# A transformer layer on one core: a new order of steps in the tail of attention, and products of ones while TensorE waits

## The chip, the cores and the metric

The kernel runs on one core of one Trainium2 chip. The metric is the device time of one execution in microseconds (us), smaller being better. PE is TensorE, DVE is VectorE, ACT is ScalarE, POOL is GpSimd and SP is SyncE, which here only starts transfers. All times in this document come from the profile of the kernel, from an answer of its trace, or from the times of whole executions.

## The reference, cut to what matters

One adaptive layer-norm block: linear attention over 2 sequences of 2048 tokens (16 heads of 16), and behind it a mixture of 8 experts of which each token wants 2, where each expert takes at most 1280 tokens, those with the largest weights first.

```python
h = _layernorm(x) * (1 + ca) + sa
x = x + ga * attention(h)        # q_feat, k_feat = elu + 1; kv = sum over tokens of k_feat x v
                                 # out = q_feat @ kv / max(q_feat @ k_sum, 1e-6) @ W_out
h = _layernorm(x) * (1 + cb) + sb
logits = xf @ router_w.T; probs = softmax(logits); topw, topi = top_k(probs, 2)
# tokens sorted by expert and weight; the first `capacity` (1280) of an expert are kept
g = einsum('ecd,edf->ecf', disp, wg); u = einsum('ecd,edf->ecf', disp, wu)
eo = einsum('ecf,efd->ecd', silu(g) * u, wd)
x = x + gb * scatter_add(eo * weight)
```

## The kernel before, in words

Every engine runs its own instruction list, written out by hand, and the lists meet at semaphores. An engine takes its instructions strictly in the order written, so an instruction that waits holds up all that stands behind it on its engine. TensorE's list, VectorE's list and so on are all emitted by a function `step(s)` of that engine, once for each step from -3 to 54. In a step each stage works on another tile of 128 tokens; there are 32 tiles (`NT`), 16 for a sequence (`TB`). The front half (layer norm, the products with `wqkv`, rotation, features, the sum `kv_ps` over keys and values) works on tile *step* or near it. The back half (called "attention proper" below) works `LAG` = 18 steps later, since it needs the sum over a whole sequence: in step *s* it does

- on PE: the transposes of `att` for tile *s*-19 (L1466), the product of `q_in` with `kvb` for tile *s*-18 (L1480), the router's product for tile *s*-21 (L1406), the output product into `y_ps` for tile *s*-19 (L1494), and the transposes of `x2` for tile *s*-20 (L1504);
- on DVE: `den_m`, `logits`, `den_r`, the greatest logits, `att` (L989), their places (`MAX_INDEX`, L883), `x2` = `y_ps` + `x_re` (L1003), and its mean and variance (L1005, L841, L846, L847);
- on ACT: the copies `attT` (L663) and `x2T` (L669) out of PSUM and the normalised tile `xn` (L678), which needs `rs2` and `sh2` from POOL;
- on POOL: `rs2` (L524), `sh2` (L526), and `xm`, `h2`.

From step 32 on only the back half is left. The second sequence's state `kvb[1]` is formed on DVE from `kv_ps` (L1033, L1035) at the end of step 33 and is first wanted by PE in step 34. The function `alone(s)` says from which step the back half has PSUM to itself: from there PE does the product L1480 ahead of the router's, the router's product gets a bank of its own, the transposes of `att` go to another bank than `y_ps` and so no longer wait for `x2`, and ACT copies `x2T` ahead of `xn` rather than behind it.

In the same steps DVE also does the softmax of the two best logits (`choice(g, part)`, parts 0 to 8) for the first 16 tiles (g = 0) and for the next 8 (g = 1). Part 0 writes `over`; ACT then takes its exponential (`exp_logits`, L608), at the end of its step `EX_STEPS`.

Behind attention stands a search with little work for PE: `choice(2, ...)` for the last 8 tiles, two transposes of the weights (L1513), 15 rounds (`DIGITS`) in which ACT and DVE count how many weights lie above a candidate (L698, L1060) and PE adds the counts over the partitions (L1518, L1520, L1522), then masks (L1533, L1534), the looking up of the chosen tokens (`look`, L1544, `place`, L1551), the gather of their rows by POOL (L556), in five parts for three groups of tiles, and their transposes (`transpose_x`, L1563). The first gate product (L1587) begins the experts, where PE is the bound.

## Time and profile before

| | us |
|---|---|
| median of 3 executions | 634.47 |
| lowest and highest | 633.26, 636.43 |
| the profiled execution | 630.97 |
| its span | 629.1 |
| granted TensorE clock in it, mean | 0.948 |
| PE busy | 559.4 (89%) |
| DVE busy | 453.0 (72%) |
| ACT busy | 322.9 (51%) |
| POOL busy | 269.9 (43%) |

The trace is that of one execution, which took 630.97 us; 1.87 us of it lie outside the span. PE's time is nearly the span, but the clock that it is granted is not full everywhere: 1.00 is 2.4 GHz and 0.50 is 1.2 GHz. So the profile is read by stretches: the front and back halves together up to about 157 us, attention proper alone up to 213 us, the search up to 264 us, and the experts.

### The profile page before, as it was taken

What the parts mean: (1) busy time and instruction counts of PE and PEld (TensorE: products, weight loads), DVE (VectorE), ACT (ScalarE), POOL (GpSimd) and SP (SyncE); (2) the same over time, 40 slices, a digit from 0 to 9 for tenths busy, and PEclk for the clock granted to TensorE, in tenths of its full rate; (3) what the DMA queues carried; (4) which work ended last, traced back from release to release, by engine and by line L of the source; (5) the groups of instructions that cost most, each with busy time, mean ns of one, the idle gap of its engine ahead of it and who ended that gap; (6) DMA issues with size and microseconds to landing.
All of it is one profiled execution on the core that took longest, in us unless ns stands there. A gap on an engine that the chain in (4) does not pass through costs nothing.

```text
span 629.1 us, 12912 instructions
## 1 busy us (share of the span) xinstructions
PE 559.4 (89%) x3895; PEld 519.9 (83%) x3895; DVE 453.0 (72%) x1357; ACT 322.9 (51%) x718; POOL 269.9 (43%) x406
## 2 busy tenths in 40 slices
PE   5999999999888532499999999999999999999993
PEld 4587779988677311399899999999999999999993
DVE  4688799998678887787577577677676776666441
ACT  4688878886334434045445454445445444454331
POOL 5788857776667600403044062070170260431321
PEclk9999999999889855599999999999999999999997
DMA  6322458644546470333637347258066174360312
GB/s 169 106 67 85 123 176 241 220 137 141 168 143 202 158 215 0 86 101 101 185 84 145 102 97 170 64 110 209 21 124 188 52 138 140 89 139 6 37 19 25
DMA packets 92480, 75.28 MB, mean 120 GB/s; under 512 B 12156, under 2 KB 89094, under 8 KB 92424
## 3 DMA queue, kind: packets, MB, share of 16 engines
q1 hardware_dynamic: 82344, 57.39, 30.5%
q0 software_dynamic: 8992, 15.90, 13.6%
q10 hardware_dynamic: 1088, 1.31, 0.7%
q8 instruction: 27, 0.44, 0.3%
q14 instruction: 29, 0.24, 0.1%
HBM read 52.41 MB, written 22.16 MB: 119 GB/s over the span
## 4 chain that ended last, share of the span: by engine, by line
PE 65%; DVE 10%; issue 4%; ACT 3%; POOL 2%; DMA 2%; SPq 0%; POOLq 0%; DVEq 0%; ACTq 0%
PE bank L1587 29%; PE bank L1601 14%; PE bank L1622 4%; PE bank L1369 4%; PE bank L1494 3%; PE bank L1637 2%; PE bank L1480 1%; PE bank L1563 1%; ACT side L698 1%; PE bank L1406 1%; DMA w_raw<-wd 1%; DVE st L1005 1%; DVE x L1003 1%; PE bank L1449 1%; PE bank L1544 1%
## 5 line engine op out<-in xcount | busy, mean ns | idle before, releaser
L556 POOL DMA_INDIRECT xg<-h_rows,g_idx x40 | 44.1, 1103 | 236.5 <-DVE g_idx L1186 226.7
L1587 PE MATMUL bank<-xT_h,w_h 128*128 128x320 f32 x448 | 139.9, 312 | 1.5 <-DVE xT_l L1215 1.5
L1587 PE MATMUL bank<-xT_l,w_h 128*128 128x320 f32 x448 | 138.4, 309 | 0.0
L1587 PE MATMUL bank<-xT_h,w_l 128*128 128x320 f32 x448 | 138.2, 309 | 0.0
L733 ACT CAST hid_h<-hid 128x320 fp32r<-128x320 f32 x112 | 51.5, 460 | 86.6 <-DVE hid L1243 86.6
L566 POOL DMA_INDIRECT out<-yo,s_idx x40 | 67.1, 1676 | 59.8 <-DVE yo L1308 26.7
L1587 PEld LDWEIGHTS bank<-xT_h,w_h 128*128 128x128 f32 x448 | 84.6, 189 | 2.2 <-issue 1.4
L729 ACT ACTIVATE act_g<-bank 128x320 f32<-128x320 f32 x112 | 49.0, 437 | 70.0 <-PE bank L1587 69.1
L1587 PEld LDWEIGHTS bank<-xT_l,w_h 128*128 128x128 f32 x448 | 84.5, 189 | 0.0
L1587 PEld LDWEIGHTS bank<-xT_h,w_l 128*128 128x128 f32 x448 | 84.4, 188 | 0.0
L1248 DVE TENSOR_TENSOR hid_l<-hid,hid_h 128x320 fp32r<-128x320 f32 x112 | 54.9, 490 | 36.5 <-ACT hid_h L733 36.1
L1601 PE MATMUL bank<-w_h,hid_h 128*128 128x256 f32 x280 | 80.2, 286 | 0.0
L1243 DVE TENSOR_TENSOR hid<-act_g,bank 128x320 f32<-128x320 f32 x112 | 54.4, 486 | 34.7 <-ACT act_g L729 33.4
L1601 PE MATMUL bank<-w_h,hid_l 128*128 128x256 f32 x280 | 78.1, 279 | 0.0
L1601 PE MATMUL bank<-w_l,hid_h 128*128 128x256 f32 x280 | 78.0, 279 | 0.0
L1201 DVE TENSOR_TENSOR w_l<-w_raw,w_h 128x768 fp32r<-128x768 f32 x64 | 61.2, 962 | 11.0 <-ACT w_h L706 10.4
L706 ACT CAST w_h<-w_raw 128x768 fp32r<-128x768 f32 x64 | 52.8, 832 | 2.1 <-DMA w_raw<-wd 2.1
L1369 PE MATMUL bank<-wqkv_h,hT_h 128*128 128x256 f32 (+1 forms) x128 | 49.0, 383 | 5.0 <-DVE hT_l L960 3.3
L1601 PEld LDWEIGHTS bank<-w_l,hid_h 128*128 128x128 f32 x280 | 52.9, 189 | 0.0
L1601 PEld LDWEIGHTS bank<-w_h,hid_l 128*128 128x128 f32 x280 | 52.8, 189 | 0.0
L1601 PEld LDWEIGHTS bank<-w_h,hid_h 128*128 128x128 f32 x280 | 52.7, 188 | 0.0
L542 POOL TENSOR_TENSOR rot<-rot_a,rot_b 128x512 f32<-128x512 f32 x32 | 42.2, 1318 | 12.4 <-DVE rot_b L953 11.9
(223 smaller groups left out, 1299.6 us busy)
## 6 DMA issues: line engine op xcount, KB each, us to landing
w_raw<-wg SPq DMA_DIRECT2D x32, 256.0 KB, 3.7
w_raw<-wu SPq DMA_DIRECT2D x32, 256.0 KB, 4.9
w_raw<-wd SPq DMA_DIRECT2D x16, 512.0 KB, 6.0
x_in<-x SPq DMA_DIRECT2D x32, 128.0 KB, 2.1
q_store<-qT SPq DMA_DIRECT2D x32, 128.0 KB, 2.1
q_in<-q_store SPq DMA_DIRECT2D x32, 128.0 KB, 2.2
x_re<-x SPq DMA_DIRECT2D x32, 128.0 KB, 2.1
out<-x SPq DMA_DIRECT2D x32, 128.0 KB, 2.1
```

Of the source, the lines that this page charges most:

```text
L542: nc.gpsimd.tensor_tensor(rot[s.par(0)][:, :], rot_a[:, :], rot_b[:, :], ALU.add).then_inc(rope_d, 1)
L556: nc.gpsimd.indirect_dma_start(out=xg[par][:, a, :], out_offset=None, in_=h2_rows, in_offset=bass.IndirectOffsetOnAxis(ap=g_idx[par][:, a: ...
L566: nc.gpsimd.indirect_dma_start(out=out_rows, out_offset=bass.IndirectOffsetOnAxis(ap=s_idx[par][:, a:a + 1], axis=0), in_=yo[:, a, :], in_ ...
L706: nc.scalar.copy(w_h[:, f, :], w_raw[:, f, :]).then_inc(sp_h, 1)
L729: nc.scalar.activation(act_g[h][:, 0:HCAP], bank[2 * h][:, 0:HCAP], ACT.Silu).then_inc(silu_d, 1)
L733: nc.scalar.copy(hid_h[f % 2][:, h * HCAP:(h + 1) * HCAP], hid[h][:, 0:HCAP]).then_inc(hh_d, 1)
L1201: V.tensor_tensor(w_l[:, f, :], w_raw[:, f, :], w_h[:, f, :].bitcast(F32), ALU.subtract).then_inc(sp_l, 1)
L1243: V.tensor_tensor(hid[h][:, 0:HCAP], act_g[h][:, 0:HCAP], bank[2 * h + 1][:, 0:HCAP], ALU.mult)\
L1248: V.tensor_tensor(hid_l[f % 2][:, h * HCAP:(h + 1) * HCAP], hid[h][:, 0:HCAP], hid_h[f % 2][:, h * HCAP:(h + 1) * HCAP].bitcast(F32), ALU. ...
L1369: ins = MM(out, x[j][:, k, :], w[i][:, k, cols], start=n == 0, stop=n == 3 * KC - 1)
L1587: last = MM(bank[2 * h + m][:, 0:HCAP], W[i][:, f, at:at + P], XT[j][:, k, cols], start=n == 0, stop=n == 3 * KC - 1)
L1601: last = MM(bank[4 + a // 2][:, a % 2 * D:(a % 2 + 1) * D], (hid_h, hid_l)[j][f % 2][:, a * P:(a + 1) * P], (w_h, w_l)[i][:, f, 4 * P:], s ...
```

## The change

1. `alone(s)` holds from step 34 (`NT + 2`) instead of step 38 (`NT + 6`).
2. The state `kvb[1]` is formed in step 33 right behind `att` instead of at the end of the step.
3. In every step of the back half `MAX_INDEX` stands behind the statistics of `x2` (`BN_STATS`) instead of ahead of `x2`.
4. The parts of `choice` stand between `BN_AGGR` and the two instructions that end the statistics, instead of at the end of the step (or between the greatest logits and `att`). The first begins in step 36 instead of 38, the second in step 44 instead of 45.
5. ACT's two `exp_logits` stand one step behind DVE's `over` instead of in the same step.
6. A new function `keep_on(b, count)` on PE issues `count` products of a 128x128 tile of ones with 512 columns of ones (bfloat16) into PSUM bank `b`, which nothing reads. 118 such products stand in PE's waits: 9 ahead of the transposes of the weights, 8 in each of rounds 0 and 8 and 3 in each of the other 13 rounds, 3 behind the rounds, 2 ahead of the first masks, 17 ahead of `look(0)`, 3 ahead of `place(0)`, 10 ahead of the second masks, 15 ahead of the first transposes of gathered rows, 1 between the first two groups of these and 3 ahead of the first gate product. None stands between the gate product and the third group.

```diff
-FIRST_CHOICE = NT + 6
-SECOND_CHOICE = NT + LAG - 5
-EX_STEPS = (FIRST_CHOICE, SECOND_CHOICE)
+FIRST_CHOICE = NT + 4
+SECOND_CHOICE = NT + LAG - 6
+EX_STEPS = (FIRST_CHOICE + 1, SECOND_CHOICE + 1)
 def alone(s):
-    return s.rep >= NT + 6
+    return s.rep >= NT + 2
...
-                    if on["logit"]:
-                        pick_places(s.t(o - 3))
+                    if s.rep == NT + 1:
+                        state(1)
...
-                    if not between(Step(s.k, s.j, s.rep + 1)):
-                        variance2(s, o)
+                if on["logit"] and on["att"]:
+                    pick_places(s.t(-LAG - 3))
+                if on["proj"] and not between(Step(s.k, s.j, s.rep + 1)):
+                    variance(st2, mv2, bn2, ag2, s.t(-LAG))
+                    if 0 <= s.rep - FIRST_CHOICE < CHOICE:
+                        choice(0, s.rep - FIRST_CHOICE)
+                    if 0 <= s.rep - SECOND_CHOICE < 3:
+                        choice(1, s.rep - SECOND_CHOICE)
...
+                    wait(dve, scale2, s.t(-LAG - 2))
+                    finish_stats(mv2, nm2[s.par(-LAG - 1)], ve2[s.par(-LAG - 1)], ag2, stat2, s.t(-LAG))
...
+            def keep_on(b, count):
+                for _ in range(count):
+                    MM(bank[b][:, :].rearrange("p (a n) -> p a n", n=P), ones_b[:, :],
+                       ones_b[:, :].unsqueeze(1).to_broadcast([P, 4, P]), start=True, stop=True)
+            keep_on(6, 9)
             pe.wait_ge(r_dve, 3)
...
+                keep_on(6, 8 if n in (0, HIGH) else 3)
                 pe.wait_ge(cnta_d, n + 1)
```

What stands where, on the engines of which the prediction speaks. PE's list in step 34, before (bank names carry no number; `x` is `x2`):

```order
L1466 MATMUL bank<-const_sb,att 128x128 [waits x2_d,att_d]
L1466 MATMUL bank<-const_sb,att 128x128
L1406 MATMUL bank<-router_c,x2T 128x8 [waits x2T_d,att_d,lgc,ld_q0,kvb_d]
L1406 MATMUL bank<-router_c,x2T 128x8
L1480 MATMUL bank<-kvb,q_in 128x136 x2
L1494 MATMUL bank<-wout_g,attT 128x256 [waits oT_d]
```

and after:

```order
L1481 MATMUL bank<-const_sb,att 128x128 [waits oT_d,att_d]
L1481 MATMUL bank<-const_sb,att 128x128
L1495 MATMUL bank<-kvb,q_in 128x136 [waits att_d,ld_q0,kvb_d]
L1495 MATMUL bank<-kvb,q_in 128x136
L1421 MATMUL bank<-router_c,x2T 128x8 [waits lgc,x2T_d]
L1421 MATMUL bank<-router_c,x2T 128x8
L1509 MATMUL bank<-wout_g,attT 128x256 [waits x2_d,oT_d]
```

The product with the state moved ahead of the router's, and the wait for `x2` moved from the transposes to the output product. Steps 35 to 37 moved in the same way; from step 38 on PE's list is the same in both.

DVE's list in step 33, before, from `att` to the state:

```order
L989 TENSOR_TENSOR att<-bank,den_r 128x256 [waits tr_o,drec]
L883 MAX_INDEX place_of<-ranked,logits 128x8 [waits max_d]
L1003 TENSOR_TENSOR x_2<-bank,x_re 128x256 [waits norm2,st_x22,tr_x2,ld_xr0,y_d]
L1005 BN_STATS st<-x_2 128x6 [waits x2_d]
L841 BN_AGGR mv<-st 128x2 [waits bn2]
L846 TENSOR_SCALAR nm_0<-mv 128x1 [waits ag2,scale2]
L847 TENSOR_SCALAR ve_0<-mv 128x1
L1033 TENSOR_TENSOR kvb<-bank,const_sb 128x2x128 [waits kv_d]
L1035 TENSOR_TENSOR kvb<-bank,const_sb 128x2x8
```

and after:

```order
L995 TENSOR_TENSOR att<-bank,den_r 128x256 [waits tr_o,drec]
L869 TENSOR_TENSOR kvb<-bank,const_sb 128x2x128 [waits kv_d]
L871 TENSOR_TENSOR kvb<-bank,const_sb 128x2x8
L1009 TENSOR_TENSOR x_2<-bank,x_re 128x256 [waits norm2,st_x22,tr_x2,ld_xr0,y_d]
L1011 BN_STATS st<-x_2 128x6 [waits x2_d]
L891 MAX_INDEX place_of<-ranked,logits 128x8 [waits max_d]
L841 BN_AGGR mv<-st 128x2 [waits bn2]
L846 TENSOR_SCALAR nm_0<-mv 128x1 [waits ag2,scale2]
L847 TENSOR_SCALAR ve_0<-mv 128x1
```

The state moved ahead of `x2` and its statistics, and the places moved from ahead of `x2` into the middle of the statistics.

PE's list in the second round of the search, after:

```order
L1539 MATMUL bank<-rows_all,ones_b 128x1 [waits won_d]
L1527 MATMUL bank<-ones_b 128x512 x3
L1542 MATMUL bank<-cnt_a,same_n 128x1 [waits cnta_d]
L1544 MATMUL bank<-cnt,same_e 128x2 [waits cnt_d]
L1539 MATMUL bank<-rows_all,ones_b 128x1 [waits won_d]
```

Only the row of L1527 is new there: three products of ones behind the round's first small product, where PE waited for ACT's count.

## Rows read from the trace of the kernel before

**Rows 1.** The page, clock granted to TensorE in 40 slices of 15.7 us, in tenths:

```profile
PEclk9999999999889855599999999999999999999997
```

**Rows 2.** Timeline, the last full steps: start us, us, engine, line, tiles [idle before]:

```profile
206.59 1.13 PE L1494 MATMUL bank<-wout_g,attT 128*128 128x256 f32 x4
207.98 0.37 ACT L669 COPY x2T<-bank 128x256 f32<-128x256 f32 x1 [1.44 <-PE bank L1504]
208.25 0.60 ACT L678 ACTIVATE xn<-x,sh,rs 128x256 f32<-128x256 f32 x1
208.75 0.36 ACT L663 COPY attT<-bank 128x256 f32<-128x256 f32 x1
209.16 1.13 PE L1494 MATMUL bank<-wout_g,attT 128*128 128x256 f32 x4
```

**Rows 3.** Timeline, DVE in one of these steps, the statistics of `x2`:

```profile
206.51 0.18 DVE L841 BATCH_NORM_AGGREGATE mv<-st 128x2 f32<-128x6 f32 x1 [0.16 <-DVE st L1005]
206.80 0.15 DVE L846 TENSOR_SCALAR nm<-mv 128x1 f32<-128x1 f32 x1
```

**Rows 4.** Timeline, steps 33 and 34, around the state of the second sequence:

```profile
156.96 1.03 PE L1494 MATMUL bank<-wout_g,attT 128*128 128x256 f32 x4
...
159.60 0.41 DVE L1033 TENSOR_TENSOR kvb<-bank,const_sb 128x256 f32<-128x256 f32 x1
...
160.15 0.61 PE L1406 MATMUL bank<-router_c,x2T 128*128 128x8 f32 x4 [1.03 <-DVE kvb L1035]
...
161.54 1.91 PE L1494 MATMUL bank<-wout_g,attT 128*128 128x256 f32 x4
```

**Rows 5.** Timeline, steps 38 and 39, around ACT's first exponential:

```profile
177.59 0.31 ACT L608 ACTIVATE ex<-over 128x128 f32<-128x128 f32 x1 [1.59 <-DVE over L893]
...
178.21 2.08 PE L1494 MATMUL bank<-wout_g,attT 128*128 128x256 f32 x4 [1.14 <-ACT attT L663]
```

**Rows 6.** Stretches: us, busy us and count of PE, PEld, DVE, ACT, POOL, clock, DMA share, GB/s:

```profile
160.00:162.00 2.00, 1.85 (x10) 1.75 (x11) 0.32 (x4) 0.60 (x1) 1.84 (x4) 0.69 0.72 241
...
214.00:216.00 2.00, 0.00 (x0) 0.00 (x0) 1.71 (x8) 1.61 (x3) 1.71 (x3) 0.85 0.19 66
```

**Rows 7.** Timeline, PE, the transposes of the weights, and two of the search's rounds:

```profile
216.60 0.69 PE L1513 MATMUL bank<-const_sb,wgt 128*128 128x128 f32 x2 [3.67 <-DVE wgt L919]
...
223.90 0.19 PE L1520 MATMUL bank<-cnt_a,same_n 128*128 128x1 bf16 x1 [0.78 <-ACT side L698]
...
232.89 0.19 PE L1520 MATMUL bank<-cnt_a,same_n 128*128 128x1 bf16 x1 [1.57 <-ACT side L698]
```

**Rows 8.** Groups by line, 216 to 266 us: busy us, mean ns | idle us before, releaser:

```profile
L1520 PE MATMUL bank<-cnt_a,same_n 128*128 128x1 bf16 x15 | 2.8, 187 | 13.1 <-ACT side L698 13.1
L1563 PE MATMUL bank<-const_sb,xg 128*128 128x128 f32 x9 | 2.6, 431 | 4.5 <-DMA xg<-h_rows,g_idx 4.5
L1544 PE MATMUL bank<-facts,onehot 128*128 128x160 bf16 x8 | 1.4, 334 | 4.7 <-DVE onehot L1160 4.7
L1533 PE MATMUL bank<-mask,before 128*128 128x32 bf16 (+1 forms) x4 | 1.0, 290 | 3.1 <-DVE mask L1104 3.1
```

**Rows 9.** The chain that ended last, 144 to 282 us: start us, us, what:

```profile
146.72 1.39 PE bank L1369 x6
...
251.22 0.73 PE bank L1544 x4
...
258.27 3.77 DMA xg<-h_rows,g_idx
...
263.79 1.94 PE bank L1587 x6
265.73 0.85 PE bank L1563 x4
266.58 0.95 PE bank L1587 x6
```

**Rows 10.** Timeline, POOL, the last of the five parts of the gather:

```profile
261.25 1.13 POOL L556 DMA_INDIRECT xg<-h_rows,g_idx  x1 [0.30 <-issue]
```

More of the change, by code:

```diff
@@ L1029, in step @@
                     mod_rows(s.rep - GATE_STEP + 1)
[L1030 to L1036 removed]
+                if s.rep == TB + 1:
+                    state(0)
             steps(dve, step, ATT)
@@ L1564, in transpose_x @@
                 last.then_inc(trx_d, 1)
+            keep_on(6, 17)
             look(0)
+            keep_on(6, 3)
             place(0)
+            keep_on(6, 10)
             pe.wait_ge(r_dve, 6)
             count_masks(1)
-            for g in range(XG - 1):
-                transpose_x(0, 0, g, first=True)
+            keep_on(2, 15)
+            transpose_x(0, 0, 0, first=True)
+            keep_on(2, 1)
+            transpose_x(0, 0, 1, first=True)
+            keep_on(2, 3)
             def gate_up(e, par, f, first=False):
```

31 lines of the change are left out of this document (18 added, 13 removed).

## The prediction

> **What bounds the kernel now.** I read the clock in slices first, then the chain that ended last, then the timeline of the places where that chain leaves PE. Of the 40 slices [rows 1] five stand out: two at 8 between 157 and 189 us, and, behind one more 8, three at 5 between 220 and 267 us. Elsewhere PE works at full clock and is nearly always busy, and nothing of the change lies there: in the steps with both halves the chain is PE alone, and the experts are PE's too. So only two stretches matter. The first is attention proper alone, from the output product of step 33 at 156.96 us to that of step 50 at 209.16 us [rows 2, 4]: 17 steps in 52.20 us, 3.07 us each. The second is the search, from the end of attention to the first activation behind the gate product at 266.58 + 0.95 = 267.53 us [rows 9]. There the chain alternates between DVE, ACT, POOL and the gather, and PE does small pieces at clock 0.50.
>
> What is the shortest step of the first stretch? Rows 2 show a loop that no DVE instruction is in. The output product of one step starts at 206.59; behind it PE does the transposes of `x2`; ACT's copy `x2T` waits for these and starts at 207.98 (1.39 later); `xn` stands behind it on ACT (0.27), `attT` behind that (0.50), and the next output product wants `attT` (0.41). The sum is 1.39 + 0.27 + 0.50 + 0.41 = 2.57 us, and it is just the distance of the two products. Order and waits of these five are the same from step 38 on before and after, so with the change no step can be shorter than 2.57 us. What the 17 steps take beyond 17 x 2.57 = 43.7 us is 8.5 us, and that is all that the first half of the change can bring.
>
> **The change, part by part.** The sum is made against the profiled execution (630.97 us, span 629.1); it is 3.5 us under the median of 634.47, and I take the difference that I find off the median.
>
> *The state.* Before, the product L1406 waits 1.03 us until `kvb` is done, which DVE forms behind `x2` and the statistics, from 159.60 us; the output product of step 34 starts at 161.54, 4.58 us after that of step 33 [rows 4]. Now the state stands right behind `att`, ahead of `x2` and its statistics, more than 1 us earlier, and PE's product with it comes ahead of the router's. It costs DVE some 0.5 us ahead of `x2`, which the output product of step 34 now waits for; that product would still start near 159.5. I take 2.5 us for this step: 2.1 us gained.
>
> *The clock in it.* Behind that stall the granted clock is 0.50 for a while (0.69 in the mean of 160 to 162 us [rows 6]), and the output product shows 1.91 us instead of 1.13 [rows 2, 4]. The same follows the stall at ACT's exponential: the product at 178.21 takes 2.08 us [rows 5]. With the stalls gone I expect the clock to stay full through both, since it stays full through all dense steps. This is inside the 8.5 us, not beyond it.
>
> *The exponential.* `exp_logits` stood in ACT's list ahead of the next `attT`, while DVE wrote `over` only at the end of its step: ACT waited 1.59 us, PE 1.14 us behind it [rows 5]. A step later `over` is long done. What is left is the instruction itself, 0.31 us on ACT and in the loop: 0.2 us for each of the two, 0.4 us, that I leave in.
>
> *`alone` from step 34.* In steps 34 to 37 the copies stand as in rows 2. No instruction is added. These steps come down to the 2.57 us of the loop.
>
> *Places and choice.* DVE waits 0.16 us between `BN_STATS` and `BN_AGGR`, and 0.29 us pass from `BN_AGGR` to the next although it is busy only 0.18 [rows 3]. `MAX_INDEX` and the parts of `choice` now lie in these gaps, worth up to 0.3 us a step on DVE. But DVE is not in the 2.57 us loop; this brings nothing of its own and only keeps DVE under 2.57 us. The statistics end later by what is put into them, 0.1 to 0.3 us, and `sh2` and `xn` with them: that chain (`x2`, statistics, POOL, `xn`, `attT`, product) covers two steps, 5.14 us, and has more than that to spare. DVE does three reductions and copies for the later look-up at the end of step 37, now as before; for them I leave 0.3 us.
>
> Sum for attention: 2.5 + 16 x 2.57 + 0.4 + 0.3 = 44.3 us instead of 52.2: **7.9 us gained**. Bounds: 8.5 if nothing is left over, 5.5 if the steps come out at 2.7 us. SP's queue moves nothing of its own; it starts four transfers a step, and they are wanted a step or two after they are started.
>
> *The products of ones.* No row shows one. The nearest at full clock is the six products of 512 columns in 1.39 us [rows 9], 0.23 us each; at half clock I take twice that less what is fixed, 0.43 us. The last activity of attention is at full clock, and 9 products follow at once: 2.1 us inside the wait of 3.67 us [rows 7]. Three in a round take 0.70 of 0.78 us; eight take 1.86 us where the second such wait is 1.57 us [rows 7], so up to 0.3 us late for the small product, but the one behind it waits for DVE anyway, and I count 0.1 us for each of the two rounds. Seventeen and three take 4.6 of 4.7 us ahead of L1544 and L1551, two and ten 2.8 of 3.1, sixteen 3.7 of 4.5 [rows 8]. So at full clock they lie in PE's waits.
>
> The Trainium skill, page "TensorE: Matmul & The Clock Gate", section "Back-to-back issue gap" and the part on 56 ns, gives 215.7 ns for 512 columns warm and 426.7 cold; rows 9 show 232 for another type. By the page eight would take 1.73 us and the two long rounds would lose next to nothing: 0.1 us less in the sum.
>
> Does the clock hold? It fell where PE did next to nothing: no product at all from 214 to 216 us, 0.85 in the mean [rows 6]. From the row at 223.90 to that at 232.89 [rows 7] lie five rounds, the last a long one, so a round takes some 1.7 us; three products give PE 0.70 us of it, more than the row before a fall shows and less than a dense step. I take it that it holds, and that where it should fall, three products at half clock would fill the round and bring it back, as the dense work behind both stalls did.
>
> *What full clock is worth in the search.* Transposes of the weights: 0.69 us for two [rows 7]; something over a third of it should go, as with the gate products below: 0.25. Rounds: the small products take 187 ns each [rows 8]; hardly any of that is columns, so between 0 and 0.1 us a round, and I take 0.03: 0.5 us. Threshold, masks and `place`: 0.25. `look`: four products in 0.73 us [rows 9], of which half: 0.3. Six gate products: 1.94 us against 0.95 us for the next six, which already ran mostly at full clock [rows 9]: 1.0. The second group's transposes give 0.25 ahead of it. The third group's, 0.85 us, would give 0.4 more, but now the gather is late: its last part starts at 261.25 [rows 10] and a part takes 3.77 us to land [rows 9], so 265.0, and full clock would want it at 264.4. So of 1.65 us in this last piece 1.25 are left. Sum: 0.25 + 0.5 + 0.25 + 0.3 + 1.25 - 0.2 = **2.4 us gained**. Bounds: 1.0 and 3.5.
>
> The experts behind it start earlier by the whole sum; their weights are started by the transposes and shift with them. 634.47 - 7.9 - 2.4 = **624.2 us** (620.7 for an execution like the profiled one).
>
> **The rivals.** *A: DVE's list is the bound, not the loop on ACT.* For: the chain of the profile runs through DVE's `x2`, statistics and places in most of these steps. Against: the products keep 2.57 us from each other to the hundredth whatever part of `choice` DVE does. If the longer statistics take over, through POOL's `rs2` and `xn`, steps of 2.8 us give 16 x 0.23 = 3.7 us back: 627.9.
>
> *B: the clock falls in the rounds or between them and comes back now and then.* Then the 2.4 us are mostly lost and some rounds are late by 0.3 us: 627.
>
> *C: the clock falls and stays low, and the products of ones are the new wait.* At 0.43 us each, three outlast the wait by about 0.35 us in 13 rounds (4.5), eight by 1.9 us twice (3.8), seventeen by 3 us, fifteen by 2.1, the others by 1: 14.4 us lost, against 7.9 gained: **641.0, slower**. It decides once the clock is low for more than half of the search (break even at 7.9 lost). Against it: at half clock PE would be some 80% busy there, and dense work at half clock got the clock back twice.
>
> *D: the change does not do what it says in attention*, as the next wait of the step is just as late (the load of `q_in`, or `x2` behind the state), so that only the two stalls' waits go, 1.0 and 1.1 us and their slow clock, some 4.5 us: 627.6.
>
> **How the numbers follow.** Forecast 0.66 at 624.2; A 0.10; B 0.12; C 0.04; D 0.05; 0.03 for anything else. The bounds of the terms give 634.47 - 8.5 - 3.5 = 622.5 and 634.47 - 5.5 - 1.0 = 628.0; medians of this kernel scatter by 1 us. With that the range is 621.5 to 628.0, which takes in B and most of A and D. 0.5%, about what a measurement can tell from no change here, is 3.2 us: faster than 631.3 in 0.93, within it 0.03, slower 0.04.
>
> **What would show it.** Right: the output products from step 34 on stand 2.57 us apart with one or two gaps of 0.2 to 0.3; no wait of PE on `kvb` or of ACT on `over` above 0.2 us; clock 1.00 from 157 us to the end; rounds that are no longer than before, with an idle time of under 0.15 us ahead of the count's product; the six gate products in 0.95 us, and behind them a wait of about 0.5 us for the gather. Wrong: steps of 2.7 us or more with ACT waiting on POOL (A); slices of 5 to 8 in the clock between 200 and 255 us (B, C); products of ones of 0.43 us, with DVE's `beats` waiting on PE (C). It would also be wrong if the experts' waits for weights, which this change doesn't touch, came out longer by what attention gave.

## The result, and the profile after

The changed kernel took **628.96 us** in the median of six executions (627.29 to 630.06), the kernel before, run beside it, 635.09 us (632.61 to 636.5). The ratio is 0.9904, with a 95% interval of 0.9877 to 0.9931: faster by 6.1 us, 4.4 to 7.8. The forecast was 10.3 us and 624.2; its range ended at 628.0. The sign was right, the size was not. Six executions more, in a later group of runs, gave 0.9904 again (0.9873 to 0.9934). One execution of q_three (1137.82 us) and one of order_gate_ones (3123.02 us), two kernels below, are left out of all medians and ratios.

The page of the changed kernel, the clock in 40 slices, against [rows 1]:

```profile
PEclk9999999999999999899999999999999999999998
```

The three 8s and the three 5s are gone; one 8 is left, at 251 to 267 us.

**Attention.** Output products of the changed kernel (they are now L1509), timeline of PE from step 33 to 39 and the last two, against [rows 2, 4, 5]:

```profile
156.50 1.03 PE L1509 MATMUL bank<-wout_g,attT 128*128 128x256 f32 x4
159.04 1.11 PE L1509 MATMUL bank<-wout_g,attT 128*128 128x256 f32 x4
161.59 1.13 PE L1509 MATMUL bank<-wout_g,attT 128*128 128x256 f32 x4
165.49 1.11 PE L1509 MATMUL bank<-wout_g,attT 128*128 128x256 f32 x4
168.04 1.13 PE L1509 MATMUL bank<-wout_g,attT 128*128 128x256 f32 x4
170.81 1.13 PE L1509 MATMUL bank<-wout_g,attT 128*128 128x256 f32 x4 [0.35 <-ACT attT L663]
173.71 1.11 PE L1509 MATMUL bank<-wout_g,attT 128*128 128x256 f32 x4
...
199.89 1.13 PE L1509 MATMUL bank<-wout_g,attT 128*128 128x256 f32 x4
202.47 1.13 PE L1509 MATMUL bank<-wout_g,attT 128*128 128x256 f32 x4
```

Step 34 follows after 2.54 us (4.58 before), and the last steps stand 2.57 us apart, as before. From step 33 to 50 it is 45.97 us instead of 52.20. But one of these steps is 3.90 us long, the one that ends at 165.49, and one further on is 2.94. What ends the idle time in them, and what SyncE's queue does just ahead (timeline of PE, then of SP; "SPq" is the time that a start takes in the queue):

```profile
164.56 0.73 PE L1495 MATMUL bank<-kvb,q_in 128*128 128x136 f32 x4 [1.41 <-DMA q_in<-q_store]
180.84 0.73 PE L1495 MATMUL bank<-kvb,q_in 128*128 128x136 f32 x4 [0.42 <-DMA q_in<-q_store]
```

```profile
159.75 2.42 SPq L402 DMA_DIRECT2D q_store<-qT  x1
162.26 0.38 SPq L385 DMA_DIRECT2D q_in<-q_store  x1
```

In the kernel before, the store of `qT` at the same place took 0.45 us to start, the load of `q_in` behind it began at 161.77 us and its product at 164.98, 3.2 us later, and no product waited for `q_in`. Here the store took 2.42 us, the load stood behind it, and PE, which now comes for it 0.9 us behind its start, waited 1.41 us. The slow start is no accident of this trace: 16 of the 17 traces, all but that of before, have one of 1.05 to 2.42 us between 159.7 and 162.9 us. ones_only below, with the old order of steps, has it too (2.29 us), and no product waits for `q_in` there. So what the new order took away is the slack behind it.

**Search.** The wait ahead of the transposes of the weights, the ones in it, and the first round, against [rows 7]:

```profile
206.09 2.10 PE L1527 MATMUL bank<-ones_b 128*128 128x512 bf16 x9
209.91 0.44 PE L1534 MATMUL bank<-const_sb,wgt 128*128 128x128 f32 x2 [1.72 <-DVE wgt L927]
210.28 0.17 PE L1539 MATMUL bank<-rows_all,ones_b 1*128 1x1 bf16 x1
210.39 1.90 PE L1527 MATMUL bank<-ones_b 128*128 128x512 bf16 x8
```

The clock is 1.00 through the rounds; a round takes 1.63 us, where it took 1.64. From these transposes to the start of the gather it is 36.95 us instead of 37.83.

**First gate product.** Timeline of PE, then two stretches (us, busy us and count of PE, PEld, DVE, ACT, POOL, clock, DMA share, GB/s), then the chain, against [rows 9]:

```profile
258.51 0.66 PE L1587 MATMUL bank<-const_sb,xg 128*128 128x128 f32 x4 [1.45 <-DMA xg<-h_rows,g_idx]
```

```profile
260.00:262.00 2.00, 1.48 (x6) 1.43 (x6) 1.93 (x5) 0.90 (x2) 0.00 (x0) 0.61 0.77 231
262.00:264.00 2.00, 2.00 (x10) 2.00 (x9) 1.32 (x3) 0.00 (x0) 0.00 (x0) 0.53 0.82 236
```

```profile
253.69 4.77 DMA xg<-h_rows,g_idx
...
260.57 3.52 PE bank L1617 x12
```

PE now waits 1.45 us for the third group of gathered rows, 1.9 us behind the end of this wait the clock falls to 0.50, and twelve gate products take 3.52 us that would take 1.9, twice the 0.95 us of [rows 9]. The first activation behind a gate product comes 13.23 us behind the gather's start (13.12 before), the second 17.26 (15.62 before). From the start of the gather to the first expert's second down product (my milestone for the end of this part) it is 27.18 us, where it was 25.73.

**The account.** Up to that milestone: attention -6.23, the search -0.88, the gate +1.45, and 0.46 us that step 33 came earlier, which the change didn't make: 280.16 us before, 274.04 after, 6.1 us. That this is the difference of the medians is luck: the profiled executions themselves differ by 2.0 us, and in the second trace of the same kernel (after_again) the same three pieces sum to 7.6 us, at the same ratio of 0.9904. Behind the milestone, where the change has nothing, the profiled execution of before took 348.9 us and that of after 353.3; in the executions below it is 348.0 to 353.8, mostly by the group of runs. In these stretches PE waits 2.2 us in the trace of before and 3.7 in that of after, none of it for weights; the rest of the 4.4 us is not explained. So the milestones are read ahead of it, and times are compared as ratios to the kernel before in the same group.

### The profile page after: what moved, and what is told of

It is laid out like the page before. It is cut to its first block, busy times and chain, and to the rows that moved or that the text cites. A ratio compares the mean times of both kernels' runs of the same rounds, so it can differ in the third digit from the quotient of the medians.

```text
span 627.3 us, 13151 instructions
## 1 busy us (share of the span) xinstructions
PE 583.7 (93%) x4013; PEld 527.4 (84%) x4013; DVE 452.5 (72%) x1357; ACT 320.4 (51%) x718; POOL 269.8 (43%) x406
## 4 chain that ended last, share of the span: by engine, by line
PE 64%; DVE 9%; issue 4%; ACT 3%; DMA 3%; POOL 2%; SPq 1%; another core or an unknown queue 1%; POOLq 0%; ACTq 0%; DVEq 0%
PE bank L1617 29%; PE bank L1631 14%; PE bank L1652 4%; PE bank L1384 4%; PE bank L1509 4%; DVE hit L1075 2%; PE bank L1667 2%; PE bank L1495 2%; PE bank L1587 1%; PE bank L1421 1%; DMA q_in<-q_store 1%; DMA w_raw<-wd 1%; POOL xg L556 1%; PE bank L1464 1%
```

## Experiments

The table has, for each trace, the output products of step 33 to 50, the transposes of the weights to the start of the gather, the gather's start to the second down product ("gate", us), and the ratio to the kernel before with its interval. Each group of runs shared one chip and its own runs of the kernel before, whose medians were 633.2 (order_only, ones_only, ones_in_gate, q_three), 630.3 (gap_filled, gate_first, round_five, dve_as_before), 633.7 (after_again to all_three) and 630.9 us (the last three).

| kernel | 33 to 50 | search | gate | ratio |
|---|---|---|---|---|
| before | 52.20 | 37.83 | 25.73 | 1 |
| changed | 45.97 | 36.95 | 27.18 | 0.9904 (0.9877 to 0.9931) |
| order_only | 45.28 | 37.84 | 26.51 | 0.9913 (0.9893 to 0.9934) |
| ones_only | 52.24 | 36.98 | 25.60 | 0.9971 (0.9951 to 0.9992) |
| ones_in_gate | 45.24 | 38.31 | 25.89 | 0.9928 (0.9905 to 0.9950) |
| q_three | 44.44 | 38.42 | 25.61 | 0.9901 (0.9875 to 0.9928) |
| gap_filled | 45.23 | 36.97 | 25.60 | 0.9917 (0.9895 to 0.9940) |
| gate_first | 44.91 | 36.96 | 25.85 | 0.9922 (0.9898 to 0.9946) |
| round_five | 45.28 | 38.68 | 25.63 | 0.9892 (0.9868 to 0.9916) |
| dve_as_before | 45.88 | 38.62 | 25.52 | 0.9909 (0.9892 to 0.9926) |
| after_again | 45.52 | 36.99 | 25.68 | 0.9904 (0.9873 to 0.9934) |
| q_no_ones | 44.76 | 37.84 | 27.83 | 0.9882 (0.9863 to 0.9901) |
| q_and_gap | 44.40 | 36.97 | 25.52 | 0.9888 (0.9862 to 0.9913) |
| all_three | 44.46 | 36.91 | 25.90 | 0.9872 (0.9849 to 0.9894) |
| q_gate_ones | 44.38 | 37.61 | 25.53 | 0.9866 (0.9843 to 0.9889) |
| q_no_ones_2 | 44.37 | 37.83 | 26.02 | 0.9894 (0.9873 to 0.9915) |
| order_gate_ones | 45.41 | 37.60 | 25.73 | 0.9878 (0.9854 to 0.9902) |

A ratio of 0.001 is 0.63 us. The intervals are 2 to 4 us wide, so most kernels with the new order can't be told from one another by time alone; the stretches of the traces can.

### The two halves of the change

order_only is the changed kernel without any of the ones:

```diff
-                for _ in range(count):
+                for _ in range(0):
```

> The changed kernel without any product of ones: the new order of steps alone. Theory (from the two profiles): the order is worth what attention gained there, 0.46 us before step 33 and 6.2 us from the output product of step 33 to that of step 50 (45.97 instead of 52.20 us), and the products of ones are worth nothing in sum, 0.9 us gained up to the gather and 1.5 us lost at the first gate products. So 6.7 us faster than before, 0.6 us faster than the changed kernel; clock 0.50 from the end of attention to the gate products, six gate products in 1.9 us, first activation 13.1 us behind the start of the gather. Rival (the forecast's own account): the ones are worth 2.4 us, so this one is only 3.7 us faster than before.

ones_only is the kernel before with the same 118 products of ones at the same places.

> The kernel before with the 118 products of ones and nothing else of the change. Theory: clock 1.00 in the search, rounds of 1.63 instead of 1.64 us, 0.9 us gained to the start of the gather, 1.5 us given back because PE idles ahead of the third group's transposes and the next gate products run at clock 0.50: 0 to 1 us slower than before, within the noise. Rival (forecast): 2.4 us faster than before. If the third group's rows land by chance earlier, the gate products keep the full clock and the gain is 1 to 2 us: then the fall hangs on the gather and not on the ones.

The order alone gives 0.9913, the ones alone 0.9971: 5.5 and 1.8 us. Together they would give 0.9884, and the changed kernel has 0.9904, which is 1.3 us less, though within what the intervals leave open. In the traces the order's part lies in attention alone (45.28 us, with the clock falling first at 208 us), the ones' part is 0.85 us in the search and 0.13 at the gate. So nearly the whole gain is the order's. Both expectations were off: the order alone was to be 0.6 us faster than the changed kernel and is not, and the ones alone were to gain nothing, or 1 to 2 us if the rows landed earlier and the clock held, and this case came about: 1.8 us, with the clock at 1.00 behind a wait of 1.16 us.

### The load of q_in

q_three gives `q_in` a third buffer and starts each load a step earlier:

```diff
-        q_in = [sa(f"q_in{i}", [P, D]) for i in range(2)]
+        q_in = [sa(f"q_in{i}", [P, D]) for i in range(3)]
...
-                    o = 1 - LAG
-                    wait(sp, o_d, s.t(o - 1))
+                    o = 2 - LAG
+                    t = s.t(o)
+                    wait(sp, o_d, t - 2)
```

> The changed kernel with three buffers for q_in instead of two, so that each load is started a step earlier. Theory: two of attention's long steps (3.90 and 2.94 us) come from loads of q_in that SP starts late, because starting a transfer of its queue took 2.4 us, and that land late; with a step more in hand both waits (1.41 and 0.42 us) go: 1.5 to 1.8 us faster than the changed kernel, output products of step 33 to 50 in 44.2 us. Rival: the transfers are late as a whole (x_re and the stores stand in the same queue), another one of them is then waited for, and the stretch stays at 46 us.

Both waits for `q_in` are gone, and attention takes 44.44 us. All six traces with the third buffer have 44.4 to 44.8 and no wait for `q_in`, all nine with the new order and two buffers 44.9 to 46.0, with one or two waits of 0.2 to 1.4 us for it. That is 0.5 to 1.6 us of the shortfall, shown in the traces. The expectation had 1.5 to 1.8 us in the time as well, and the time of q_three is no better (0.9901): its search is 1.5 us longer, which is the next point. Over all four pairs of kernels that differ in the third buffer alone the ratio is lower with it (0.9901 and 0.9904, 0.9882 and 0.9913, 0.9888 and 0.9917, 0.9866 and 0.9878), 1.2 us in the mean; no pair shows it by itself, and two of them are from different groups.

### The clock behind attention

Timeline of q_three, PE and the first round's count on DVE, where the changed kernel has 1.90 us for the same eight ones:

```profile
209.25 0.44 PE L1537 MATMUL bank<-const_sb,wgt 128*128 128x128 f32 x2 [1.72 <-DVE wgt L929]
209.62 0.17 PE L1542 MATMUL bank<-rows_all,ones_b 1*128 1x1 bf16 x1
209.73 3.41 PE L1530 MATMUL bank<-ones_b 128*128 128x512 bf16 x8
212.93 0.21 PE L1545 MATMUL bank<-cnt_a,same_n 128*128 128x1 bf16 x1
...
213.28 0.16 DVE L1085 SCALAR_TENSOR_TENSOR beats<-bank,unit 128x3 f32<-128x3 f32 x1 [1.47 <-PE bank L1547]
```

PE stood still for 1.72 us ahead of the transposes, the clock fell to 0.50 from 210 to 213 us, and the eight ones, at 0.43 us each, were the thing that DVE waited for: 1.47 us. The Trainium skill, page "TensorE: Matmul & The Clock Gate", section "Wait — 56ns, not 53.3ns?", has 426.7 ns cold and 215.7 ns warm from one product of 512 columns to the next. The traces agree: these eight took 3.41 us, eight times 0.426, and the nine in the changed kernel 2.10 us, nine times 0.216 and 0.16 for the last to end.

gap_filled sets 16 ones into this wait instead of 9.

```diff
-            keep_on(6, 9)
+            keep_on(6, 16)
```

> The changed kernel with 16 products of ones instead of 9 between the last router product and the transposes of the weights. In the traces of the changed kernel with a third q_in buffer and of the one with more ones at the gate, PE idles 1.72 us there as in the changed kernel itself, but the granted clock falls to 0.50 right behind it, and the 8 ones ahead of the first round take 3.4 and 3.3 us instead of 1.9: DVE waits 1.47 us for PE. 16 products at 0.216 us are 3.46 us of a wait of 3.82. Theory 1 (what PE does not do in this gap lets the clock go): the clock stays at 1.00 at 209 to 216 us, first round's count without that wait, transposes of the weights to gather 36.9 to 37.0 us (37.84 without any ones), and the time 0 to 1.4 us under the changed kernel's, depending on how often that one falls there. Theory 2 (the fall comes from what ran before the gap, not from it): the fall is seen here too, 38.3 us, and the time is the changed kernel's. Theory 3 (the ones outlast the wait): the transposes of the weights start later than 7.44 us behind the last output product.

```profile
205.55 3.61 PE L1527 MATMUL bank<-ones_b 128*128 128x512 bf16 x16
209.38 0.44 PE L1534 MATMUL bank<-const_sb,wgt 128*128 128x128 f32 x2 [0.22 <-DVE wgt L927]
```

The idle time is 0.22 us, the clock stays at 1.00, and the search takes 36.97 us. The ratio, 0.9917, is not under the changed kernel's 0.9904, where 0 to 1.4 us less had been expected. q_and_gap has both edits and shows the same (44.40 and 36.97).

> The changed kernel with a third q_in buffer and with 16 ones instead of 9 ahead of the transposes of the weights. Theory 1 (the gap of 1.7 us lets the clock go, and 16 ones close it): clock 1.00 from 206 to 216 us, transposes of the weights to gather 36.97, attention from step 33 to 50 in 44.45, second down product 25.6 to 25.7 us behind the gather's start, together 7.75 + 0.87 + 0.1 = 8.7 us under the kernel before at that product and a ratio of 0.986 to 0.988. Theory 2 (the clock falls by chance, with 16 ones too): 38.4 us here, ratio 0.989.

Its ratio, 0.9888, lies above the expected 0.986 to 0.988 and is not below that of the same kernel without any ones, 0.9882. And all_three, with 16 ones here too, shows the limit of the cure.

> The kernel with a third q_in buffer and 16 ones ahead of the transposes of the weights, and in the first gate product 8 ones ahead of the third group's transposes and 3 behind the next six products. Theory 1 (the clock at the gate holds anyway in most executions; ones there cost a little): second down product 25.6 to 25.9 us behind the gather's start, ratio as the kernel without these 11 ones, within 0.002. Theory 2 (the clock falls at the gate in many executions and costs 1.5 us each time): ratio lower by 0.001 to 0.002.

Stretches of all_three, and PE in it:

```profile
202.00:204.00 2.00, 1.54 (x8) 1.15 (x8) 1.37 (x6) 0.63 (x2) 1.57 (x4) 1.00 0.39 131
204.00:206.00 2.00, 1.54 (x10) 1.20 (x10) 1.53 (x12) 0.98 (x3) 1.85 (x4) 0.61 0.16 56
206.00:208.00 2.00, 2.00 (x7) 0.82 (x7) 1.44 (x8) 0.92 (x3) 1.78 (x3) 0.50 0.25 84
```

```profile
206.11 6.15 PE L1530 MATMUL bank<-ones_b 128*128 128x512 bf16 x16
```

Here the clock fell at 204.4 us, still in attention's last two steps, ahead of any of the ones. The 16 then took 6.15 us instead of 3.61 and ended 2.7 us after the weights were there: the transposes came 10.11 us behind the last output product, not 7.44. That is the mechanism of rival C, once instead of everywhere. The 11 ones at the gate, for which this kernel was made, show nothing: the clock held there, the milestone is at 25.90, and 0.9872 and 0.9888 can't be told apart. after_again is the changed kernel unchanged:

> The changed kernel once more, unchanged. Of the seven traces with the new order and 9 ones ahead of the transposes of the weights, three have the clock at 1.00 behind them and four at 0.50 for 3 us, in which the 8 ones ahead of the first round delay it by 1.4 us. Theory: ratio to the kernel before 0.990 to 0.992; in the trace, transposes of the weights to gather is either 36.95 or 38.4 us and nothing between, and the second down product lies either 25.6 or 27.2 us behind the gather's start. The rival, that the four falls belong to the small edits of those four kernels, would give 36.95 here.

Its search is 36.99 us, and its clock is 1.00 all the way from 140 to 272 us, where the other trace of the same kernel has the fall at 260 us. That fits the theory and its rival alike, since here it named 36.95 for both. (Among the seven traces that the expectation counts is ones_only, which has the old order.) With this one seven traces have the new order and 9 ones in this wait: three hold the clock at 1.00 there (changed, after_again, gate_first), and four have it at 0.50 for 3 to 7 us (q_three, ones_in_gate, round_five, dve_as_before). q_three and dve_as_before also change what runs ahead of it. But the other five have the same instruction lists up to the end of the first round, and 1.72 or 1.73 us of idle time ahead of the transposes: three hold and two fall. So the same work with the same wait can keep the clock or lose it. In dve_as_before the fall came at 208.6 us, while PE was busy with the nine ones, and in all_three ahead of any, so the wait of 1.72 us is not the cause in every trace; and that 16 ones prevent the fall is not shown by two traces that hold and one that does not.

The times point the same way, though not in every kernel. In gap_filled the mean granted clock of the six executions was 0.994, 0.994, 0.992, 0.992, 0.991 and 0.988, and their times 622.4, 622.8, 624.6, 625.2, 626.1 and 626.7 us. From 0.994 to 0.988 is 0.006 x 621 / 0.5 = 7.5 us more at half clock. Work bound by PE would lose half of that, 3.7 us, and the time is 4.3 us longer, as if the clock fell where PE is waited for. In after_again the lowest clock, 0.985, goes with the longest execution, 631.1 us, too. This is read from how clock and time go together in a few executions and not from an experiment; in q_and_gap an execution with 0.990 took 623.5 us and that with the highest clock, 0.995, 625.4, and order_only, without any ones, scatters as much (625.5 to 630.2), so there is another source as well.

### What the ones return

round_five has five ones in a short round instead of three.

```diff
-                keep_on(6, 8 if n in (0, HIGH) else 3)
+                keep_on(6, 8 if n in (0, HIGH) else 5)
```

> The changed kernel with five ones in each of the twelve short rounds instead of three. Three took 0.82 us and the round 1.63, with 0.26 us of idle time ahead of the next product. Theory 1 (a product of ones costs nothing until it outlasts the wait, then its whole length): five are 5 x 0.216 = 1.08 us plus 0.17, 0.43 more than three, of which 0.2 to 0.3 lie in the wait and the rest delays the count: a round of 1.75 to 1.9 us, and with 12 rounds 1.5 to 3 us later at the gather. Theory 2 (PE's reading runs beside VectorE's and takes its time from it): a round grows by less than 0.1. The time is 1.5 to 3 us over the changed kernel's by theory 1, within 0.7 us by theory 2.

A round took 1.65 us instead of 1.63, where theory 1 had 1.75 to 1.9, and the ratio, 0.9892, is no higher than the changed kernel's: five ones just fit. Timeline of one of its rounds:

```profile
216.06 1.25 PE L1527 MATMUL bank<-ones_b 128*128 128x512 bf16 x5
216.19 0.48 DVE L1075 TENSOR_SCALAR_CACHE_REDUCE hit<-val,cand 128x256 bf16<-128x256 f32 x1
216.25 0.51 ACT L698 ACTIVATE side<-val,cand 128x256 bf16<-128x256 f32 x1 [1.05 <-DVE cand L1087]
...
216.60 0.48 DVE L1075 TENSOR_SCALAR_CACHE_REDUCE hit<-val,cand 128x256 bf16<-128x256 f32 x1
...
217.15 0.17 PE L1542 MATMUL bank<-cnt_a,same_n 128*128 128x1 bf16 x1
217.18 0.16 PE L1544 MATMUL bank<-cnt,same_e 128*128 128x2 bf16 x1
217.38 0.16 DVE L1083 SCALAR_TENSOR_TENSOR beats<-bank,unit 128x3 f32<-128x3 f32 x1 [0.22 <-PE bank L1544]
```

A round is `cand`, two `hit`, and the small product L1544 that waits for the second, with the ones of 1.25 us beside the two `hit`. The clock shortens the small product from 187 ns [rows 8] to 176 in the mean of the changed kernel, and that is all that it can give in a round. (The fall of the last section is in this trace too; its search is 38.68 us.)

dve_as_before undoes a part of the new order on VectorE: `pick_places` stands ahead of `x2` again and the parts of `choice` behind the statistics. It is less than its expectation says. The state stays right behind these places and ahead of `x2`, and the choices begin in their new steps and are spread as in the changed kernel.

> The changed kernel with VectorE's work of attention as the kernel before has it: the places of the largest logits and the choice in their old positions, the state's step behind them. Only the order on PE and ScalarE is new. Theory 1 (the loop of 2.57 us is x2's, through ScalarE and PE, and VectorE has slack): output products stay 2.57 us apart, but the state's step is again late where VectorE makes kvb behind the choice, 0.5 to 1.1 us at the third step, and attention from step 33 to 50 takes 46.5 to 47.5 us instead of 46.0. Theory 2 (VectorE's order is what made the steps short): steps return to 2.9 to 3.7 us and attention to 50 us or more. Times: 629 to 630.5 by theory 1, 632 or more by theory 2, where the kernel before is 635.1.

Attention took 45.88 us, with most steps at 2.55 to 2.67. Less the 0.64 us by which the third step is long for `q_in` it is 45.24, 0.8 more than with the third buffer, and the transposes of the weights come 0.17 us later behind the last output product. So the new positions of places and choice are worth 1.0 us by this reckoning; the rest, 6.8 of the 7.8 us that the new order has where `q_in` does not wait, is in the place of the state on VectorE, the order on PE and ScalarE and the steps at which the choices and exponentials stand. No run parts these. The expected 46.5 to 47.5 us rested on a late state, which this kernel does not have (its first step is 2.67 us).

### The first gate product

> The changed kernel with 8 more products of ones between the first six gate products and the transposes of the third group, and 3 behind the next six, where PE idled 1.45 and 0.52 us. Theory: the clock falls there because PE idles, so now it stays 1.00 and the twelve gate products behind take 1.8 instead of 3.52 us: 1.7 us faster than the changed kernel, 7.8 us faster than before. Rival: the fall has its cause earlier or elsewhere (the clock still falls near the gate products), no gain; or the eight (1.73 us) end behind the gather's landing and cost some 0.1 to 0.3 us of it.

> The changed kernel with the transposes of the first expert's third group of rows behind the gate products of both halves' first slice instead of ahead of the first half's second, their two copies moved behind the work that they now follow, and 4 and 3 ones around them. In the changed kernel PE waits 1.45 us for these rows at 258.5 us with the first half's other products ready behind them, and the clock falls after. Theory 1 (rows' landing is the term that was missed): no wait for xg there, clock at 1.00 through 264 us, first down product 19.3 to 20.0 us behind the gather's start instead of 21.1, second under 26, and the time 1.2 to 2.4 us under the changed kernel's. Theory 2 (the clock's fall alone costs, the wait for rows is covered): as the kernel with ones around the wait, second down product at 25.9, no more. Theory 3: the two copies move the wait on to ScalarE or VectorE and the second down product is no earlier than 27.2.

The two edits, ones around the wait, and the transposes put behind the second half's products:

```diff
                         if first and (h, m) == (0, 0):
+                            keep_on(2, 8)
                             transpose_x(0, 0, XG - 1, first=True)
+                        if first and (h, m) == (0, 1):
+                            keep_on(2, 3)
```

```diff
-                        if first and (h, m) == (0, 0):
-                            transpose_x(0, 0, XG - 1, first=True)
...
+                    if first and h == 0:
+                        keep_on(2, GAP)
+                        transpose_x(0, 0, XG - 1, first=True)
+                        keep_on(2, 3 if GAP else 0)
```

The clock held at the gate in both, and neither is faster for it: 0.9928 and 0.9922, where 1.7 and 1.2 to 2.4 us under the changed kernel's time had been expected. (ones_in_gate has the fall of the clock at 211 us, with a search of 38.31 us, so its time says little of the gate.) But in eight traces without either edit it held too (ones_only, q_three, gap_filled, round_five, dve_as_before, after_again, q_gate_ones, order_gate_ones), and there the milestone is at 25.5 to 25.7 us. In q_and_gap it was low from 254.8 to 258.2 us, while the rows were still on their way, and that cost nothing (25.52). The edits cost 0.2 us against these. gate_first has no wait for the rows and its first activation at 11.15 us, 2 us earlier than the others, and its chain shows why that brings nothing: from 257.75 us to the transposed list at 271.88 it runs mostly through VectorE, through the description of the other rows (`in_block`, `facts`, `onehot`) and the first copies of the next weights, with twelve gate products (2.04 us) and some copies of ScalarE between. In the kernel before the third transposes come 11.09 us behind the gather's start with PE at half clock and without a wait; at full clock in gap_filled 11.43 us, with a wait:

```profile
257.78 0.66 PE L1587 MATMUL bank<-const_sb,xg 128*128 128x128 f32 x4 [1.18 <-DMA xg<-h_rows,g_idx]
```

PE is ready earlier, and the rows are not. Full clock is worth 0.1 us here. Three traces in which the clock is low in this part are later than before: by 1.5 (changed), 0.8 (order_only) and 2.1 us (q_no_ones, where it lasts until 264.5 us):

> The changed kernel with a third q_in buffer and without any of the ones: the new order alone with its two waits for q_in taken away. Theory 1 (order and buffer carry the gain, the ones some 0.9 us of it where the clock holds and a loss where it falls): attention from step 33 to 50 in 44.4 to 44.5 us, transposes of the weights to gather 37.84, second down product 26 to 26.5 us behind the gather's start, ratio 0.988 to 0.991. Theory 2 (the ones carry it): ratio 0.993 or more.

There attention took 44.76 us, since PE also waited in three steps for VectorE's `att`, 0.20 to 0.36 us each. The milestone at 27.83 is later than either theory had it; the ratio of 0.9882 is the one that theory 1 gives.

### Ones only ahead of the gate

The last three kernels have ones only behind the last round, where a fall has no more rounds to delay; the nine ahead of the transposes and those in the rounds are left out. q_gate_ones has the third `q_in` buffer, order_gate_ones has not.

```diff
-            keep_on(6, 9)
...
-                keep_on(6, 8 if n in (0, HIGH) else 3)
```

> The changed kernel with a third q_in buffer, and with ones only behind the last round of the search: none ahead of the transposes of the weights and none in the rounds. Theory 1 (ones in the rounds return little and delay work when the clock has fallen; those ahead of the gate return the 2 us by which the same kernel without ones has its second down product later, 27.8 instead of 25.6 us behind the gather's start): transposes of the weights to gather 37.4 to 37.8 us, second down product 25.5 to 25.9 behind the gather's start, no loss ahead of the rounds, ratio 0.985 to 0.988, under that of the same kernel with no ones (0.9882). Theory 2 (the trace's 2 us at the gate do not reach the end, as the times of the kernels with and without ones suggest): ratio 0.988 or more.

> The kernel with the new order and the third q_in buffer and without ones, once more, beside the one with ones only ahead of the gate. Theory 1 (its second down product lies at 26.5 to 27.8 us behind the gather's start in every execution, since the clock stays low until the gate products themselves raise it): a ratio of 0.988 to 0.990 and 1 to 3 us over the kernel with ones ahead of the gate. Theory 2: the two are the same within 1 us.

> The changed kernel with ones only behind the last round of the search: none ahead of the transposes of the weights and none in the rounds, q_in as in the changed kernel. Theory 1 (as above): against the changed kernel's 0.9904 the same or lower by up to 0.002, since it gives up 0.6 us of the search and has no ones that can run at half clock ahead of the first round, which cost 1.4 us in four of the seven traces with 9 ones. Theory 2 (the ones ahead of the rounds are needed): 0.992 or more, transposes of the weights to gather 38.4 us or more.

Stretches of q_gate_ones around the end of the rounds, and the gate:

```profile
236.00:238.00 2.00, 2.00 (x11) 0.97 (x11) 0.83 (x6) 2.00 (x4) 0.00 (x0) 0.50 0.00 0
238.00:240.00 2.00, 2.00 (x9) 0.73 (x8) 1.79 (x10) 1.03 (x2) 0.00 (x0) 0.73 0.03 8
240.00:242.00 2.00, 2.00 (x11) 0.94 (x10) 2.00 (x5) 0.00 (x0) 0.00 (x0) 1.00 0.00 0
```

The clock is 0.50 from 205 to 239 us and costs 0.64 us of the search (37.61 against 36.97); it comes back while seventeen ones in a row run, and it holds at the gate (25.53). This is the lowest ratio of all: 622.68 us (621.37 to 623.08) against 630.9, 0.9866, 8.2 us under the kernel before. The same without any ones has 0.9894, 1.3 us more, with a milestone of 26.02 instead of 26.5 to 27.8. The two intervals overlap, and the same kernel had 0.9882 in another group; but in this group the longest of the five executions with these ones (623.08 us) is shorter than the shortest of the six without (623.38). order_gate_ones has 0.9878, where the changed kernel had 0.9904 twice. The intervals overlap: that the ones ahead of the rounds and in them cost more than they give is likely by these runs, and not shown. What is shown is that leaving them out loses nothing that can be measured.

## Why the prediction was wrong

**The 2.57 us loop: right.** Steps without another wait are 2.53 to 2.59 us in every trace with the new order of PE, ScalarE and VectorE. The new positions of places and choice keep VectorE out of the loop and give 1.0 us by that; with the old ones (dve_as_before) PE waits for `att` in five steps. Rival A (DVE's list as the bound) is out, but for the three steps of q_no_ones.

**The stalls at the state and at the exponential: right.** Step 34 follows after 2.54 us, the waits on `kvb` and `over` are gone, and the clock is 1.00 through both. The 0.4 us that I left for the exponentials and 0.3 for the reductions are there: three steps of 2.77, 2.9 and 2.72 us, 0.7 more than 3 x 2.57. With the third buffer attention took 44.4 us, where the forecast had 44.3.

**"SP's queue moves nothing of its own; it starts four transfers a step, and they are wanted a step or two after they are started": this step failed.** I had given the next wait on `q_in` a chance of 0.05, as rival D, and there with nothing between "all steps late" and "none". The load of `q_in` waits in SP's queue behind the store of `qT` (or, in the ninth step, behind the load of `x_re` and two stores). Starts there take up to 2.42 us, a load takes 2.2 us to land (median of this stretch), PE wants it a step later, and the two steps ahead of the third had become 2.0 and 1.4 us shorter. The third step is long by 0.2 to 1.35 us and the ninth by up to 1.0, together 0.5 to 1.6 us: of 7.9 us 6.2 came in the profiled execution.

**The gate's 1.25 us: this term failed, by 1.1 to 2.7 us.** I let the last part of the gather land 3.77 us after its start, from a row of another part, and set it off against full clock with 0.4 us. It took 4.77 us in the changed kernel and 4.54 in gap_filled. So PE's wait was 1.0 to 1.45 us where the clock was full, not 0.6, and with the clock holding the gain is 0.1. I also took what PE gains there for gained in the end, and it is not: gate_first has its first activation 2 us earlier and its milestone no earlier, since VectorE's chain decides. In the profiled execution the clock didn't hold, and the experts' start lost 1.45 us instead of winning 1.25. It fell 1.9 us behind the wait that I had named as harmless; but behind waits of 1.0 to 1.3 us at the same place it held in eight traces, so whether the wait brought the fall stays open.

**The rounds' 0.5 us: mis-sized.** They gave 0.01 us each, 0.15 in all. With the transposes, threshold, masks and look-up the search gave 0.88 us of the 1.1 forecast there; those small terms were right.

**That the clock holds: right in the rounds, wrong around them.** Three ones in a round kept it at 1.00 in every trace in which it was 1.00 when they began. That three would also bring it back, as the forecast had it, no trace shows: where it had fallen, it came back while the eight of the first round ran or within 0.5 us of their end, ahead of the next ones, and in all_three while the 16 ran. But I looked only for waits without any ones and overlooked two: the 1.7 us that nine ones leave of the 3.8 ahead of the transposes, and the end of attention itself, where in all_three the clock fell with PE still at its last steps (busy 1.54 of 2 us). Rival B had a clock that falls now and then in the rounds or between them, with 627 us and a chance of 0.12. Falls now and then are what happened, but around the rounds, together with D's wait for `q_in`. With both as measured in the profiled execution the sum is 634.47 - 6.23 - 0.88 + 1.45 = 628.8 us, and I had them as alternatives. That it meets the median of 628.96 is luck in part, as said at the account: in after_again the clock held, the wait for `q_in` was shorter, and the ratio is the same. The cause of that remainder, some 1.5 us, stays open.

**Rival C** (ones at half clock as the new wait) happened too, but for single waits: some 1.4 us in the first round of four traces, 2.7 in all_three. The clock was back within 3 to 7 us.

**The sign for the experts** (longer waits for weights): not seen. PE waits for no weights behind the milestone in either trace.

## What to carry to other kernels

When a loop gets shorter, list every transfer that it waits for and how long before its use it is started: the slack of an old step is not that of a new one, and here one buffer more took away what the shorter loop had brought up, 0.5 to 1.6 us. Look for the return of filler products in work that is bound by PE: in the rounds here, which wait for ACT and VectorE, they returned 0.01 us a round. And if the clock happens to be low when they start, they take twice their length and delay what stands behind. The lowest ratio here had them only in the last stretch ahead of the dense work, though it can't be told from the 0.9872 of all_three, which has them everywhere. Add up waits that can happen in the same execution instead of holding them against each other as rivals.

## What was not expected of the hardware

- The start of one transfer on SP's queue took 2.42 us and another 1.28, where the same starts took 0.45 and 0.33 us elsewhere in the same trace; the transfers are 128 KB each, and the profile doesn't show what held them. A start of 1.05 to 2.42 us stands at nearly the same time, 159.7 to 162.9 us, in 16 of 17 traces, but not always at the same transfer.
- The place at which the clock falls changes from one execution of the same kernel to the next, or it doesn't fall at all: with the same instruction lists ahead of it, it fell at 210.7 and 211.2 us in two traces and not in three others. With the ones in every wait the mean clock went from 0.95 to 0.99 and the time by 0 to 2 us.
- The last of five parts of an indirect gather landed 4.5 to 4.9 us after its start where PE waited for it, while an earlier part needed 3.8 [rows 9]; in the kernel before, where PE came 4.3 us behind the start, it was already there.
